# Placing the split queries of three cross-attention layers with selection matmuls instead of a trip through DRAM

## The reference, cut to what matters

```python
q = _split_heads(query @ wq_kernel + wq_bias)      # 256 queries, 16 heads of 16
k = _split_heads(key @ wk_kernel + wk_bias)        # 4096 keys
scores = jnp.einsum('bhqd,bhkd->bhqk', q, k) / jnp.sqrt(jnp.float32(HD))
...                                                # layer 1 masks by (query, key)
attn = jax.nn.softmax(scores, axis=-1)
out = jnp.einsum('bhqk,bhkd->bhqd', attn, v)
out = out.transpose(0, 2, 1, 3).reshape(b, -1, D)
return out @ wo_kernel + wo_bias
```

## Time and profile before

| | |
|---|---|
| time, median of 3 runs | 1492.37 us (1487.21 to 1492.59) |
| profiled execution, its own time | 1488.9 us |
| its span | 1487.5 us |
| mean granted TensorE clock | 0.963 of full speed |
| PE busy | 1356.0 us (91%) |
| DVE busy | 1005.1 us (68%) |
| ACT busy | 859.9 us (58%) |
| POOL busy | 568.7 us (38%) |

### The profile page before, as it was taken

The page is one execution under the profiler, slowest core; times in us unless marked ns, Lnnn a source line. Parts: engine busy times, 40 slices in busy tenths (PEclk is TensorE's granted clock), DMA queues, the critical chain, the costliest instruction groups (busy, mean ns, idle before and its releaser), DMA issues. The chain is left out here.

```text
span 1487.5 us, 28822 instructions
## 1 busy us (share of the span) xinstructions
PE 1356.0 (91%) x10423; PEld 802.3 (54%) x10496; DVE 1005.1 (68%) x2324; ACT 859.9 (58%) x1326; POOL 568.7 (38%) x686
## 2 busy tenths in 40 slices
PE   8999798999999988799999788699999896999987
PEld 3765656355555456355555554255555582555555
DVE  4445485999999734778787143588885337888832
ACT  5143141899999731388888552167777302777762
POOL 4565252688989920655555340111110001111100
PEclk9999999899999998899999999799999997999999
DMA  8877997246547053266655195257776711677700
GB/s 274 286 266 250 246 256 261 47 65 87 75 69 161 2 81 48 57 93 92 85 82 146 34 212 201 80 79 104 103 112 196 111 18 46 97 108 104 152 2 8
DMA packets 126008, 178.30 MB, mean 120 GB/s; under 512 B 14733, under 2 KB 106021, under 8 KB 116646
## 3 DMA queue, kind: packets, MB, share of 16 engines
q1 hardware_dynamic: 111898, 161.04, 52.9%
q10 hardware_dynamic: 13968, 15.41, 3.4%
HBM read 132.58 MB, written 43.78 MB: 119 GB/s over the span
## 5 line engine op out<-in xcount | busy, mean ns | idle before, releaser
L1046 ACT ACTIVATE prob_a<-ps 128x1024 f32<-128x1024 f32 x464 | 456.6, 1020 | 143.5 <-PE ps L878 95.4
L861 PE MATMUL ps<-kop,qop 116*128 116x512 bf16 x1024 | 345.4, 401 | 34.8 <-DMA qop<-qparts 21.8
L1070 DVE TENSOR_REDUCE best_a<-ps 128x1 f32<-128x512 f32 (+1 forms) x488 | 318.4, 709 | 49.4 <-PE ps L861 49.0
L878 PE MATMUL ps<-qop,kop 116*128 116x256 bf16 x2048 | 333.9, 274 | 7.7 <-ACT prob_a L1046 3.1
L878 PEld LDWEIGHTS ps<-qop,kop 116*128 116x128 bf16 x2048 | 193.8, 98 | 124.7 <-ACT prob_a L1046 21.9
L1066 DVE CUSTOM_DVE_ANT_0 dump_a<-ps,neg_q 128x512 bf16<-128x512 f32 (+1 forms) x244 | 165.9, 715 | 44.3 <-PE ps L861 42.2
L905 PE MATMUL ps<-prob_a,vop_a 128*32 128x256 f32 x3072 | 191.7, 383 | 3.1 <-POOL prob_a L1210 2.2
L861 PEld LDWEIGHTS ps<-kop,qop 116*128 116x128 bf16 x1024 | 95.2, 103 | 160.3 <-issue 64.3
L1180 POOL TENSOR_TENSOR used_a<-prob_a,gT 128x1024 f32<-128x1024 f32 x64 | 154.4, 2414 | 22.1 <-DVE used_a L1083 17.0
L1159 POOL CAST mpart_a<-nmax_a 128x2 bf16<-128x2 f32 x64 | 26.3, 411 | 348.1 <-DVE nmax_a L1075 348.1
L1210 POOL TENSOR_TENSOR prob_a<-prob_a,neg_k 128x1024 f32<-128x1024 f32 x48 | 102.5, 2135 | 92.8 <-ACT prob_a L1044 86.3
(11 more groups left out here) (333 smaller groups left out, 1768.0 us busy)
## 6 DMA issues: line engine op xcount, KB each, us to landing
kop<-kparts SPq DMA_DIRECT2D x448, 128.0 KB, 5.2
kparts<-kp SPq DMA_DIRECT2D x64, 384.0 KB, 4.7
vals<-vst SPq DMA_DIRECT2D x16, 1024.0 KB, 5.2
vraw<-vals SPq DMA_DIRECT2D x64, 256.0 KB, 6.6
e_w<-in_e_w SPq DMA_DIRECT2D x4, 2048.0 KB, 10.8
z_w<-in_z_w SPq DMA_DIRECT2D x24, 256.0 KB, 7.0
ctxT<-in_ctxT SPq DMA_DIRECT2D x8, 512.0 KB, 8.0
raw<-in_mask ACTq DMA_DIRECT2D x16, 256.0 KB, 5.3
```

The costliest lines, as they stand in the source:

```text
L861: return pe.matmul(out, qop[0:R_ALL, h, t * P:(t + 1) * P], kop[0:R_ALL, h % UNROLL, j * CHUNK:(j + 1) * CHUNK], start=True, stop=True)
L878: ins = pe.matmul(st_bank(n)[:, j * NT:(j + 1) * NT], kop[0:R_ALL, h % UNROLL, k * P:(k + 1) * P], qop[0:R_ALL, h, :], start=(j % 2 == 0), ...
L1046: act.activation(prob[:, n % NP, :], st_bank(n), ACT.Exp).then_inc(S("exp_done"), 1)
L1070: dve.tensor_reduce(out, bank, AX.X, ALU.max).then_inc(sem, 1)
```

## The change

Six things change, all for layers 1 to 3; layer 0 keeps its path.

1. The stores to and loads from `qparts` go, and the DMA for the mask row in layer 2 with them.
2. A selection tile `sel` is built on DVE in each of the three layers: one memset and seven copies of 16-column pieces of the identity (`select`). It takes the place of the memset of `qop`.
3. PE forms each head's 116 rows with three matmuls of 256 columns, one per part, that add up in PSUM (`spread`), in banks 2 and 7 alternately.
4. ACT copies each head's 116 rows from PSUM to `qop` (`place`), sixteen copies per layer; in layer 2 with a bias that makes the mask row one.
5. Head 0 is spread before the opening, heads 1 to 15 within it: two heads behind the score matmuls of each step from 2 on. Score matmuls wait for the copy of their head, and PE waits for all 16 copies ahead of `turn_max`.
6. After the projection PE runs `SPLIT_FILL` = 7 idle matmuls in layers 2 and 3. The projection writes banks 5 and 6 in place of 1 and 2. The weights of the queries are laid out without the turn within heads that the DRAM path needed.

```diff
+SPREAD_BANKS = (2, 7)
+SPLIT_FILL = 7
...
+    def select(self, dve, S):
+
+        dve.memset(self.sel[:, :, :, :], 0.0).then_inc(S("sel_cleared"), 1)
+        dve.wait_ge(S("sel_cleared"), 1)
+        heads = self.c.identb[:, :].rearrange("p (g e) -> p g e", e=HD)
+        for at, (_, part) in zip(ROW_AT, PAIRS):
+            dve.tensor_copy(self.sel[:, :, part, at:at + HD], heads).then_inc(S("sel_set"), 1)
+
+    def spread_out(self, h):
+
+        return self.c.ps[0:R_ALL, SPREAD_BANKS[h % 2], 0:NT]
+
+    def spread(self, pe, S, h):
+
+        mt, g = divmod(h, H // CT)
+        if h == 0:
+            pe.wait_ge(S("sel_set"), len(PAIRS))
+        pe.wait_ge(S("q_part2"), mt + 1)
+        if h == 1 and self.l == SHIELDED:
+            pe.wait_ge(S("blind_found"), 1)
+        if h >= 2:
+            pe.wait_ge(S("q_placed"), h - 1)
+        for part in range(3):
+            ins = pe.matmul(self.spread_out(h), self.sel[:, g, part, :], self.half(self.qp[:, part, :], mt),
+                            start=(part == 0), stop=(part == 2))
+        ins.then_inc(S("q_spread"), 1)
+
+    def place(self, act, S):
+
+        for h in range(H):
+            act.wait_ge(S("q_spread"), h + 1)
+            if self.l == KEYED:
+                act.activation(self.c.qop[0:R_ALL, h, :], self.spread_out(h), ACT.Identity,
+                               bias=self.c.ident[0:R_ALL, R_MASK:R_MASK + 1]).then_inc(S("q_placed"), 1)
+            else:
+                act.activation(self.c.qop[0:R_ALL, h, :], self.spread_out(h), ACT.Copy).then_inc(S("q_placed"), 1)
...
-    banks = (1, 2)
+    banks = (5, 6)
...
-        dve.memset(c.qop[96:P, :, :], 0.0).then_inc(S("qop_set"), 1)
+        q.select(dve, S)
         q.rest_and_third(dve, S, banks)
...
             sum_masks(pe, MASKS_FIRST, KT).then_inc(S("masks_summed"), 1)
+        else:
+            keep_warm(c, pe, SPLIT_FILL)
...
-        q.load_half(act, S, 1)
+        q.place(act, S)
...
-        q.store(sp, S)
-        q.load_half(sp, S, 0)
-        q.load_rest(sp)
...
-            pe.wait_ge(ops.S("q_first" if h < UNROLL else "q_rest"), Q_DONE * (l + 1))
+            if asked is not None:
+                pe.wait_ge(asked.S("q_placed"), h + 1)
+            else:
+                pe.wait_ge(ops.S("q_first" if h < UNROLL else "q_rest"), Q_DONE)
...
+        if asked is not None:
+            asked.q.spread(pe, asked.S, 0)
         for n in range(FIRST):
...
+            if n == 2 and asked is not None:
+                pe.wait_ge(asked.S("q_rested"), CT)
...
+            if asked is not None and n >= 2:
+                for h in (2 * n - 3, 2 * n - 2):
+                    if h < H:
+                        asked.q.spread(pe, asked.S, h)
             if n == SC // 2 + 2:
+                if asked is not None:
+                    pe.wait_ge(asked.S("q_placed"), H)
                 turn_max(0)
```

More of the change, by code:

```diff
@@ L311, with __init__ @@
 class QueryParts:
-    def __init__(self, c, l, rest, qp):
-        self.c, self.l, self.rest, self.qp = c, l, rest, qp
+    def __init__(self, c, l, rest, qp, sel=None):
+        self.c, self.l, self.rest, self.qp, self.sel = c, l, rest, qp, sel
     def half(self, tile, mt):
@@ L711, in queries @@
     sb = lambda name, shape, dt: ctx.enter_context(c.nc.sbuf_tensor(f"{name}_q{l}", shape, dt))
-    q = QueryParts(c, l, sb("qrest", [P, CT * NT], F32), sb("qp", [P, 3, CT * NT], BF16))
+    q = QueryParts(c, l, sb("qrest", [P, CT * NT], F32), sb("qp", [P, 3, CT * NT], BF16),
+                   sb("sel", [P, H // CT, 3, R_ALL], BF16))
     warm = sb("warm", [P, 1], F32)
-    banks = (1, 2)
+    banks = (5, 6)
     blind = sb("blind", [P, NT], BF16) if l == SHIELDED else None
     stage = Stage(S)
-    stage.blind = blind
+    stage.blind, stage.q = blind, q
     @stage.vector
@@ L836, in _ @@
             load_next(sp)
-        if l == KEYED:
-            sp.wait_ge(asked.S("mask_placed"), 16)
     @stage.tensor
@@ L2718, in lay_out @@
     turned_heads = lambda a: np.ascontiguousarray(a.reshape(*a.shape[:-1], H, HD).swapaxes(-1, -2).reshape(a.shape))
-    out["wq4"] = turned_heads(out["wq4"])
+    out["wq4"] = np.concatenate([turned_heads(out["wq4"][:1]), out["wq4"][1:]])
     out["bk4"] = np.ascontiguousarray(stack(bias["k"]).reshape(LAYERS, CT, P).transpose(2, 0, 1))
@@ L2756, in lay_out @@
     out["g_b1"] = np.ascontiguousarray(i["L3_ffn_b1"].reshape(-1, P).T)
-    bq = np.stack([turned_heads(i[n]) for n in bias["q"]])
+    bq = np.stack([turned_heads(i[n]) if n == bias["q"][0] else i[n] for n in bias["q"]])
     out["bq4"] = np.ascontiguousarray(bq.reshape(LAYERS, CT, P).transpose(2, 0, 1))
```

## The result

The changed kernel takes 1476.45 us, the median of 5 runs (1474.77 to 1481.06), where the kernel before took 1489.23 in 5 runs (1487.21 to 1492.59) made with them: 12.8 us less by the medians. The ratio of the runs is 0.9894, with a 95% interval of 0.9869 to 0.9920. That is faster, by 0.8 to 1.3%; the prediction said 1477.0.

The account below looks back on a forecast made before the run. It took PE's DRAM waits (21.8 us), DVE's reductions in the openings and PE in the steady part as bounds. Gains 6.1 + 5.8 + 1.4 = 13.3 us took 1488.9 to 1475.6; forecast 1477, range 1472 to 1485.

Parts of the forecast that it names:

- First score in layers 2 and 3: Start of the opening in layers 2 and 3: the first score matmul comes 5.5 and 5.2 us earlier.
- Selection tile: DVE's building of `sel`: memset 1.20 us, seven copies 1.2 (ends 0.4 and 2.0); 0.1 us charged.
- Clock: PE's granted clock lasts at 1.00, bringing DVE's first reduction in layers 2 and 3 0.45 us further forward.
- Opening: Steps 2 to 9: DVE's 1.14 us hides PE's 1.10; 116-column weight loads charged at 0.3 us a layer.
- First group of keys: Four matmuls behind the opening in layers 2 and 3: full clock gains 0.4 us, with PE the bound from here.
- Layer 1: POOL's `find_seen` holds up the split of head 0's maximum, so layer 1 gains 1.4 us, ends 1.1 and 3.
- the loads that do not overlap: Rival, opening: each spread matmul waits for its own weight load, a step takes 1.86 us; 1487, chance 0.05.
- The cold opening: Rival, opening: PE at half clock, a step takes 2.1 us, eight steps lose 7.9; 1497, chance 0.05.
- The two banks: Rival, opening: a bank's loop of 1.4 us a step loses 2.1 us a layer; 1480, chance 0.10.

Follow-up runs that it names:

- experiment 4: Kernel before, with idle matmuls while PE waits for the queries from DRAM (26, 37 and 36 in layers 1 to 3): 1488.00 us, ratio 0.9991 to the kernel before.
- experiment 5: Changed kernel with a selection tile of 128 columns in place of 116: 1474.22 us in one run.
- experiment 6: Changed kernel with each head's three spread matmuls done twice: 1483.87 us, against 1478.73 for the changed kernel on the same chip.
- experiment 3: Changed kernel with POOL's split of head 0's maximum ahead of find_seen's third group in layer 1: 1471.91 us; again, 1472.35 against the changed kernel's 1478.73 on one chip.
- the second execution: The changed kernel profiled once more, with nothing changed, on one chip with follow-up runs: 1478.73 us.
- experiment 8: The kernel before once more, with nothing changed, for its stage lengths in a second profiled execution: 1487.49 us.
- experiment 7: Changed kernel with no idle matmuls in the query stages of layers 2 and 3, neither during norm nor split: 1481.44 us, ratio 0.9936 to the kernel before.

## Why the prediction was right

The time, 1477 against 1476.45, was right, and most terms were too. That it came within 1 us is partly luck: the three layers gained 13.1 us between the first two profiles, where 13.3 was forecast, but 11.2 over both executions of each kernel.

- *First score in layers 2 and 3.* 5.5 and 5.2 us earlier were forecast, 13.15 - 7.66 = 5.5 and 12.71 - 7.54 = 5.2 measured. The chain's prices held: three matmuls 0.51 (0.49 forecast), copy 0.47 and 0.38.
- *Selection tile.* The memset took 1.22 (1.20), seven copies 1.23 (1.2, between ends of 0.4 and 2.0). The charge of 0.1 us wasn't there: the rest of the split began 4.66 us after the norm in both kernels.
- *Clock.* It stayed at 1.00 through the openings, and the first reduction came 5.9 and 5.6 us earlier, the 0.45 more than the first score. Experiment 4 adds what the forecast didn't say: on the old path a full clock at the start did not last; with the spread matmuls between the scores it did.
- *Opening.* The charge of 0.3 us a layer was not there either: the first group of keys is 5.9 and 5.6 us earlier, exactly the first reduction's advance. The slow loads are real (131 ns, as 126 against 98 had suggested) and stretched a step to 1.17 in layer 2, but PE's lead covers that (experiments 5 and 6).
- *First group of keys.* The 0.4 us for the full clock is the term that was mis-sized. The group took 0.61 us in place of 1.03, but the stretches of layers 2 and 3 shrank by 5.9 and 5.6 us, no more than the group had moved. "PE is the bound from here" was wrong: from 958 to 970 us DVE was busy 11.93 of 12.00 us and PE 8.69, so DVE's reductions still set the pace. Forecast were 6.1 and 5.8. This 0.4 and the charges of 0.1 and 0.3 cancelled; the sum was right partly for that.
- *Layer 1.* 1.4 us forecast, 27.96 - 26.54 = 1.4 measured at the first group of keys, 1.6 in the stretch, and 1.0 over both executions of each kernel. POOL was the gate as said, and experiment 3 shows it by moving it. But the chain to the gate begins ahead of POOL: in the second execution the projection at half clock held up the mask's sums and `blind`, `find_seen` started 10.2 us after the norm instead of 8.6, and the first group of keys came at 28.07, no earlier than before. That the stretch came out near 1.4 is luck too. The turn of the last head's maximum is 227.99 - 225.35 = 2.6 us earlier, and behind the cross attention PE ran some 4 us at half clock, where the kernel before had 1.00; the step behind the cross attention took 62.38 us instead of 60.80:

```profile
876.00:880.00 4.00, 3.86 (x22) 2.49 (x22) 0.56 (x1) 2.17 (x10) 1.60 (x4) 0.57 1.02 163
```

Of the rivals, the loads that do not overlap fell with the step of 1.13 to 1.17 us, where 1.86 was their price. The Trainium skill has that rule in "TensorE: Matmul & The Clock Gate", in a bullet of the section "The mechanism" of Part 3; the trace disagrees: three matmuls in the same rows, each with a load of 131 ns, took 0.51 us, so each followed the last after 0.12. Its rule that the fast weight load needs 128 weights, in "Weight-path perf modes" of the same page, the trace bears out, with 131 ns against 96. The cold opening does not hold: even when forced it lasted four steps, about two of the eight with spread matmuls. Its sum was also too dear by the lead of 2 to 3 us a layer. The two banks set no pace that showed in the time. The times of these first two rivals were counted from 1488.9 us, the forecast from 1.4 us more.

What stays open: why the granted clock was at half in the projections of layers 1 and 3 in one execution of the changed kernel and not in the other, with the same instructions, and why it fell behind layer 1's cross attention in the first. Nor do these runs say why layer 0, which the change doesn't touch, took 3.3 us longer in one execution of the kernel before than in the other.

## What to carry to other kernels

When an engine waits for a short trip through DRAM, price the whole chain that can replace it, and then put only the first piece of it ahead of the consumer: here one head of sixteen is on the path, and the same work in one piece would have made the kernel slower than before. Work that is hidden behind a paced engine has two covers, the difference of the steps and the lead that the buffers hold; count both before you pay for a shorter step. When a stage is brought forward, look at what is queued ahead of the next hand-over on each engine: in layer 1 three quarters of the gain to be had at the first group of keys (4.0 of 5.4 us) hung on the order of two pieces of POOL's work, neither of which the change touched. And keep an eye on the clock ahead of the stage that you changed: a projection at half clock cost as much as layer 1 had gained.

## What the runs showed of the hardware that I had not expected

- PE's granted clock fell to 0.50 within an opening that had begun at 1.00 with full idle matmuls before it, when only two score matmuls of 0.60 us stood in each 1.13 us (experiment 4). With six spread matmuls more in each step it stayed at 1.00.
- An opening that began at 0.50 was at 1.00 some 5 us later, on the spread matmuls and scores alone (experiment 7).
- The same projection, with the same 2.10 us of standing ahead of its stage, took 1.99 us in one execution, and 2.42 or 3.78 in another, where the granted clock was 0.50 for part or all of it (experiment 8).
- A bfloat16 weight load of 116 columns took 131 ns at the median and one of 128 columns 96 ns; the longer one, between matmuls of 0.11 us, added 0.02 to a step of 1.14 in layer 2 (experiment 5).
